# Moving VectorE's gate from step 1 to step 2 of a selective scan, and ScalarE's PSUM copies ahead of the decay of their step

## The reference, cut to what matters

```python
xz = x @ in_w.T;  xi, z = split(xz)
xi = silu(conv1d(xi) + conv_b)
dt, Bm, Cm = split(xi @ xp_w.T)
delta = softplus(dt @ dt_w.T + dt_b)
h[t] = exp(delta*A)[t] * h[t-1] + (delta*Bm*xi)[t]     # scan over 1024 positions
y = sum_s(h * Cm) + xi * Dp
y = y * silu(z)                                       # the gate
out = y @ out_w.T
```

## Time and profile before

| | before |
|---|---|
| median of 3 runs | 5113.8 us (5072.42 to 5123.27) |
| the profiled execution | 5129.01 us |
| its span | 5127.2 us |
| mean granted TensorE clock | 0.867 of full |
| busy: PE, DVE, ACT, POOL | 4297.8, 3660.3, 2793.5, 2334.3 us |
| DVE idle ahead of the gate (L1267), 64 gates | 166.2 us |
| PE idle ahead of u (L692) waiting for a scan | 169.9 us, 89 times |

### The profile page before, as it was taken

The page is one execution under the profiler, slowest core; times in us unless marked ns, Lnnn a source line. Parts: engine busy times, 40 slices in busy tenths (PEclk is TensorE's granted clock), DMA queues, the critical chain, the costliest instruction groups (busy, mean ns, idle before and its releaser), DMA issues.

```text
span 5127.2 us, 48989 instructions
## 1 busy us (share of the span) xinstructions
PE 4297.8 (84%) x14248; PEld 1563.2 (30%) x14248; DVE 3660.3 (71%) x3157; ACT 2793.5 (54%) x3396; POOL 2334.3 (46%) x1084
## 2 busy tenths in 40 slices
PE   6779986999869998699876998779987799868887
PEld 2322233222332223322233222332233222332223
DVE  1468865798547886498855987658876689657886
ACT  2556545565555655465465664555546556455453
POOL 0146631566315663166622665236642366315563
PEclk9889987898878989799897998878998799977778
DMA  1156631666216652276523665146641566305551
GB/s 37 38 132 161 160 90 37 161 163 151 67 39 159 168 147 60 69 169 154 130 77 74 170 158 129 42 105 144 165 120 39 121 165 157 98 12 144 133 140 46
DMA packets 166840, 580.30 MB, mean 113 GB/s; under 512 B 22460, under 2 KB 23208, under 8 KB 162952
## 3 DMA queue, kind: packets, MB, share of 16 engines
q1 hardware_dynamic: 152168, 538.66, 43.0%
q10 hardware_dynamic: 14336, 37.76, 2.5%
HBM read 467.12 MB, written 71.48 MB: 105 GB/s over the span
## 4 chain that ended last, share of the span: by engine, by line
issue 33%; POOL 27%; PE 22%; ACT 9%; DVE 7%; DMA 1%; POOLq 0%; SPq 0%; DVEq 0%; ACTq 0%
POOL arena L1371 25%; PE ps L496 3%; PE ps L551 3%; PE ps L592 2%; PE ps L711 2%; ACT arena L816 2%; PE ps L542 2%; PE ps L646 1%; ACT arena L834 1%; POOL arena L1361 1%; PE ps L692 1%; DVE arena L1282 1%; PE ps L570 1%; PE ps L526 1%; POOL x L1379 1%
## 5 line engine op out<-in xcount | busy, mean ns | idle before, releaser
L1371 POOL TENSOR_TENSOR arena<-arena 128x1024 f32<-128x1024 f32 x768 | 1858.6, 2420 | 1218.6 <-DVE arena L1282 1218.6
L1282 DVE TENSOR_TENSOR_SCAN arena<-arena,ps 128x1024 f32<-128x1024 f32 x768 | 1755.9, 2286 | 101.4 <-ACT arena L985 3.8
L985 ACT ACTIVATE arena<-arena,a_all 128x1024 f32<-128x1024 f32 x768 | 872.4, 1143 | 599.0 <-DVE arena L1282 489.2
L692 PE MATMUL ps<-arena,spread 32*128 32x512 f32 x1536 | 947.0, 705 | 220.2 <-DVE arena L1282 169.9
L1277 DVE TENSOR_TENSOR ps<-ps,arena 128x1024 f32<-128x1024 f32 x768 | 934.5, 1217 | 267.9 <-PE ps L694 267.1
L694 PE MATMUL ps<-arena,spread 32*128 32x512 f32 x1536 | 933.5, 706 | 0.0
L711 PE MATMUL ps<-arena,gather 128*32 128x512 f32 x3072 | 566.8, 679 | 40.4 <-POOL arena L1371 40.4
L692 PEld LDWEIGHTS ps<-arena,spread 32*128 32x128 f32 x1536 | 244.6, 199 | 892.6 <-issue 527.9
L757 PE MATMUL ps<-x 96*96 96x512 f32 x1008 | 502.8, 617 | 0.0
L646 PE MATMUL ps<-arena,w_in 96*96 96x512 f32 x512 | 315.8, 774 | 65.7 <-DMA arena<-xq 65.7
L1325 POOL TENSOR_TENSOR x<-x,arena 96x512 f32<-96x512 f32 x64 | 109.4, 1709 | 434.5 <-DVE arena L1121 434.5
(11 more groups left out here) (158 smaller groups left out, 5666.3 us busy)
## 6 DMA issues: line engine op xcount, KB each, us to landing
arena<-dl SPq DMA_DIRECT2D x768, 512.0 KB, 4.8
dl<-arena ACTq DMA_DIRECT2D x64, 384.0 KB, 4.7
x<-pn SPq DMA_DIRECT2D x56, 247.5 KB, 4.8
arena<-in_x SPq DMA_DIRECT2D x9, 1536.0 KB, 10.7
arena<-xq SPq DMA_DIRECT2D x64, 192.0 KB, 7.2
arena<-arena ACTq DMA_DIRECT2D x64, 192.0 KB, 6.2
out<-x SPq DMA_DIRECT2D x64, 192.0 KB, 2.1
arena<-xq SPq DMA_DIRECT2D x64, 191.8 KB, 6.8
```

Source lines behind the costliest of these rows:

```text
L692: pe.matmul(ps[:, bank, :], spread[rows[0], r, :], u[rows[0], i, 0:512], start=True, stop=True)
L985: act.activation(da[:, m % DAS, :], dbc[:, m % DBC, :], ACT.Exp, scale=a_all[:, v // 2, m:m + 1]).then_inc(da_ready, 1)
L1282: dve.tensor_tensor_scan(hs[:, m % HSS, :], da[:, m % DAS, :], driven, 0.0, ALU.mult, ALU.add).then_inc(h_ready, 1)
L1371: pool.tensor_tensor(product, product, cmat[:, v % 2, :], ALU.mult).then_inc(pr_ready, 1)
```

## The change

The gate of unit v - 1 is issued on DVE behind the scan of step 2 and not of step 1. On ACT the copies of B and C and the projection's copy now stand ahead of the decay that is issued in the same step. The four delta activations get new step numbers and the place ahead of the decay; step 3 behind the decay and step 4 ahead of it are the same place in ACT's queue, so their order is what it was. The two DMA issues of ACT (L968, L977) stay behind the decay. No instruction, operand or wait is added or removed. In the preparation of unit 0, which has no decays between, ACT's order stays as it is.

```diff
-ACT_DT, ACT_B, ACT_C, ACT_OUT = (3, 4), (6, 7), (8, 9), (10, 11)
+ACT_DT, ACT_B, ACT_C, ACT_OUT = (4, 5), (6, 7), (8, 9), (10, 11)
-S_GATE, S_SKIP = 1, 3
+S_GATE, S_SKIP = 2, 3
...
-        def scan_stage(prep, first, step, conv, last):
+        def scan_stage(prep, first, step, conv, last, early=lambda slot, v: None):
 
             for slot in range(G):
+                early(slot, 0)
                 prep(slot, 0)
             first()
             for v in range(UNITS):
                 for m in range(G):
+                    if v + 1 < UNITS:
+                        early(m, v + 1)
                     step(v, m)
                     conv(m, v)
                     if v + 1 < UNITS:
                         prep(m, v + 1)
...
-                def prep(slot, v):
+                def early(slot, v):
...
+                    if slot in ACT_DT:
...
+                    if slot in ACT_B:
+                        c = ACT_B.index(slot)
+                        act.wait_ge(b_ps, 2 * V + c + 1)
+                        if v >= 2 and c == 0:
+                            act.wait_ge(bu_ready, (V - 1) * G)
+                        act.activation(part(bmat[:, i, :], c), ps[:, bank(c), :], ACT.Copy).then_inc(b_ready, 1)
+                    if slot in ACT_C:
...
                 def step(v, m):
                     w, k = after(v, m, DAS - 1)
+                    if m in ACT_OUT and v >= 2 and v % 2 == 0:
+                        copy_out(v // 2 - 1, ACT_OUT.index(m), 6)
                     if w < UNITS:
                         decay(w, k)
-                    if m in ACT_OUT and v >= 2 and v % 2 == 0:
-                        copy_out(v // 2 - 1, ACT_OUT.index(m), 6)
...
-                scan_stage(prep, first, step, conv, final)
+                scan_stage(prep, first, step, conv, final, early)
```

More of the change, by code:

```diff
@@ L919, in pair @@
                                    ACT.Identity, bias=ln_wb[:, 1:2], scale=ln_wb[:, 0:1]).then_inc(pix_act, 1)
+                part = lambda t, c: t[:, c * 512:(c + 1) * 512]
+                def early(slot, v):
+                    V = p * UNITS + v
+                    q, i = divmod(v, 2)
+                    bank = lambda c: 6 + c if v == 0 else 6
+                    if slot in ACT_DT:
+                        c = ACT_DT.index(slot)
+                        bias = small_all[:, q, KC + 1:KC + 2]
+                        act.wait_ge(dt_ready, 2 * V + c + 1)
+                        if v and c == 0:
+                            act.wait_ge(delta_ready, V)
+                        act.activation(part(soft, c), ps[0:DI, bank(c), :], ACT.Abs,
+                                       bias=bias).then_inc(soft_act, 1)
+                        if v and c == 0:
+                            act.wait_ge(u_ready, V)
+                            act.wait_ge(delta_out, V * 16)
+                        act.activation(part(delta, c), ps[0:DI, bank(c), :], ACT.Relu,
+                                       bias=bias).then_inc(soft_act, 1)
+                    if slot in ACT_B:
[5 more added lines that the diff above has]
+                    if slot in ACT_C:
+                        c = ACT_C.index(slot)
+                        act.wait_ge(c_ps, 2 * V + c + 1)
+                        if v >= 2 and c == 0:
+                            act.wait_ge(pr_ready, (V - 1) * G)
+                        act.activation(part(cmat[:, i, :], c), ps[:, bank(c), :], ACT.Copy).then_inc(c_ready, 1)
                 def prep(slot, v):
@@ L924, in prep @@
                     q, i = divmod(v, 2)
-                    bank = lambda c: 6 + c if v == 0 else 6
-                    part = lambda t, c: t[:, c * 512:(c + 1) * 512]
                     if slot == ACT_SILU:
@@ L941, in prep @@
                         exp_table()
[L942 to L954, removed]
                     if slot == ACT_SOFT:
@@ L959, in prep @@
                         act.activation(soft, soft, ACT.Ln, bias=eps[0:DI, 2:3]).then_inc(soft_act, 1)
[L960 to L965, removed]
                     if slot == ACT_DL:
@@ L968, in prep @@
                         act.dma_start(a["dl"][i], delta).then_inc(delta_out, 16)
[L969 to L974, removed]
                     if slot == ACT_U:
```

## The result

The changed kernel takes 4865.1 us (median of 5 runs, 4861.6 to 4889.3) against 5111.5 us (5 runs); the ratio is 0.955, with a 95% interval of 0.952 to 0.958. It is the slowest of the five, 24 us above their median, so waits read from its trace are somewhat longer than the typical ones.

What follows compares the result with a forecast made beforehand. A loop of TensorE's sum, gate, multiply 2, scan 2 and u(4), with the clock falling behind its wait, was taken as the bound; 78 + 63 + 44 = 185 us gave 4930 us, range 4860 to 5045.

Steps and rivals of the forecast that it cites:

- rival 2: TensorE stays at full clock nearly throughout and only the floors remain: 4832 us; chance 0.07.
- Term A: VectorE's 56 moved gates: the wait for TensorE's sum goes, up to about 1.98 us each; 78 us.
- Term B: Steps 5 and 6: without TensorE's wait at u(4) the clock stays up; 63 us, bounds 0 and 84.
- Rival 1: Only the direct wait is won, the clock falls as often: 5036 us, 5000 to 5063; chance 0.17.
- Term C: Unit's end, steps 9, 10, 11 and 0: half of 88 us of waits for u goes; 44 us, bounds 0 and 64.
- ScalarE's copies ahead of the decay: ScalarE's queue: TensorE waits less for B's copy in the last pair, 0 to 10 us; cost taken as 0.
- ScalarE's Silu of z: ScalarE's queue: Silu waits for the later gate, but decay 4 keeps 1.1 us of cover before scan 4; price 0.

Runs made afterwards that it cites:

- the DMA moved alone: Kernel before with the gate behind scan 2 and the DMA of u's lower half issued ahead of decay 11 and C's second copy; 4865.5 us, ratio 0.956.
- the wait put back: Changed kernel with TensorE's u(4) waiting for VectorE's multiply of step 3 in units 1 to 7; 4979.6 us, ratio 0.979.
- the copy put back: Changed kernel with the second copy of C at step 9 back behind its decay; 4932.2 us, ratio 0.969.

## Why the prediction was right, and where not

- **The range and the sign** held: 4865 lies in 4860 to 5045, near its lower end. It lies below the 4875 to 4985 that the prediction held for most likely, in the part that it had taken in for rival 2. The forecast of 4930 was 65 us too slow; 185 us were predicted of the profiled execution, 240 came.
- **Term A, the gate's wait**: 78 us, "in any case". Measured 117.1 less 43.1 of new waits of multiply 2, 74 us (39 expected there, in 15 gates; by the trace they are 20). The wait did move to multiply 2 as worked out, but the size isn't independent of the rest: with the gate alone multiply 2 waits 74.9 us, which leaves 42, and with the DMA moved alone 23.8, which leaves 93. The closeness of 78 and 74 is partly luck.
- **Term B, clock and steps 5 and 6**: 63 us, with three quarters assumed. Measured 82.6, nearly all of the 84.5. Its cause is shown from both sides: the wait put back brings the low clock back, the wait filled removes it. Rival 1, by which the clock would fall all the same, is refuted by 1.00 in 42 stretches. So the rule of thumb on idle gaps of the Trainium skill, TensorE: Matmul & The Clock Gate, section "HAM oscillation — how this bites in real kernels", doesn't hold for these rows, in which the clock fell behind waits of 1.94 to 2.42 us. The section on micro-idles of the same page of the Trainium skill comes nearer, but it speaks of frequent ones, and here one in a unit of some 48 us was enough in 34 of 42.
- **Term C, the end of the unit**: 44 us of 88. Measured 52, but with the gate alone it is 32 (88 to 56). What made up the difference isn't in its reasoning, but in the step that follows.
- **The failed step** is "ScalarE's copies ahead of the decay", with "I take 0" and a price of 0 to 10 us. The copies themselves are indeed worth nothing. But behind the second copy of C stood a DMA, and with the gate moved its place was worth 76 us. The prediction saw that a broadcast of delta in SyncE's queue goes out later by this order and counted that as a possible cost; it left out ScalarE's own DMA, which lands 1.6 us sooner for it (6.09 for 7.72 in the table above). In VectorE's waits the difference between the gate alone and the whole change stands at multiply 2 (74.9 to 43.1 us) and at steps 9 to 0 (56 to 36). That the total came out near is partly luck: the same 185 us would have been predicted for the gate alone, which brings 3.0%, 155 us of 5111.5.
- **ScalarE's Silu of z**: 1.1 us of cover and a price of 0. Right: the scan waits 1.0 us in all, and one step later the wait is 2.3 us where this working gives 2.4.
- **Signs in the profile**: gate 48.7 us as named (49); TensorE's wait for scan 2 down from 130 to 14 us; clock 0.95 to 0.99 in seven stretches, but 0.82 in the last pair, for which above 0.85 was named; 2229 us for "near 2270"; waits of 2 us and more at multiply 2 in 14 units for "some ten"; TensorE's wait for a copy of B 1.1 us at the longest where 1.5 was named. The 19 us that VectorE was busy less weren't in the sum.

## What to carry to other kernels

A wait in a loop can cost more than its own length: the moved gates had waited 117 us, and moving them alone brought 155. Follow the wait to TensorE, look at the granted clock behind it, and price both. When instructions change places in a queue, list everything that moves relative to anything else, the DMA issues of that queue above all; here the order of a copy of 0.6 us and a decay, with neither the transfer of 192 KB nor its wait touched, decided over 76 us, because the decay let a broadcast of 512 KB go out ahead of that transfer. And a step has room on both sides: bound the next place as well, since one step further the whole gain was gone.

## What the runs showed of the hardware that I had not expected

- Needless matmuls make the kernel faster, by 0.9%, where they fill a wait of 1.94 us and hold the granted clock at 1.00 instead of 0.75 in the 10 us behind it.
- The same wait doesn't lower the clock each time: in 34 of 42 stretches of the kernel before and in 22 of 42 with the wait put back. Behind the wait of 1.4 us at u(8) it was 12 of 42, behind that of 3.1 us at the skip product 42 of 42. These stand at different places, and what decides in the single unit was not tried.
- A transfer of 192 KB landed in a median of 2.9 to 3.0 us in the kernels that mostly issued it ahead of all three broadcasts of delta (46 to 49 of 56 units), of 5.5 us in the changed kernel (behind two of them in 49 of 56), and of 6.9 to 7.0 us with the gate alone and with the copy put back (behind all three in 33 and 28 of 56).
